# A perceiver layer with eight experts: conditional loads of the experts' low weight parts

## The reference

```python
expert_weight, expert_idx = jax.lax.top_k(probs, TOP_K)      # 2 of 8 experts for each of 2048 rows
...
binned = jnp.zeros((E, cap, Cc), x.dtype).at[sorted_e, local_pos].set(x[sorted_tok])
inter = jnp.einsum('ecd,efd->ecf', binned, w1_stack)
inter = jnp.square(jax.nn.relu(inter))
outb = jnp.einsum('ecf,edf->ecd', inter, w2_stack)
flat_out = outb[sorted_e, local_pos] * sorted_w[:, None]
moe_out = jnp.zeros((t, Cc), x.dtype).at[sorted_tok].add(flat_out)
return shared_out + moe_out
```

## Time and profile before

| | us |
|---|---|
| median of 3 runs (1295.1 to 1296.33) | 1295.25 |
| the profiled execution | 1296.94 |
| its span from first to last instruction | 1295.2 |
| TensorE busy | 1268.2 |
| VectorE busy | 749.9 |
| the routed groups, from about | 986 |
| to the last inner product of a group, about | 1230 |
| DMA traffic, whole kernel | 391.42 MB |

### The profile page before, as it was taken

The page is one execution under the profiler, slowest core; times in us unless marked ns, Lnnn a source line. Parts: engine busy times, 40 slices in busy tenths (PEclk is TensorE's granted clock), DMA queues, the critical chain, the costliest instruction groups (busy, mean ns, idle before and its releaser), DMA issues.

```text
span 1295.2 us, 21508 instructions
## 1 busy us (share of the span) xinstructions
PE 1268.2 (98%) x7571; PEld 829.1 (64%) x7572; DVE 749.9 (58%) x1404; ACT 358.0 (28%) x632; POOL 168.6 (13%) x173
## 2 busy tenths in 40 slices
PE   6999999999999999999999999999998999999999
PEld 3444444444444444467888888899986677777743
DVE  4456566554554545468878888666434444444456
ACT  2312212221121211326444444532312323223200
POOL 1000000000000000003100004504324000000054
PEclk9999999999999999999999999999999999999999
DMA  9999999999999999803467752223689898998897
GB/s 358 411 419 416 414 416 418 418 419 419 419 419 412 400 391 394 324 18 149 169 253 272 293 216 78 92 72 123 234 291 305 280 298 293 310 307 289 281 348 250
DMA packets 119699, 391.42 MB, mean 302 GB/s; under 512 B 11744, under 2 KB 34272, under 8 KB 115424
## 3 DMA queue, kind: packets, MB, share of 16 engines
q1 hardware_dynamic: 114528, 374.00, 76.3%
q0 software_dynamic: 5120, 16.78, 3.6%
HBM read 332.54 MB, written 58.20 MB: 302 GB/s over the span
## 4 chain that ended last, share of the span: by engine, by line
PE 92%; DMA 4%; DVE 2%; issue 1%; SPq 1%; ACT 0%; POOL 0%; ACTq 0%; POOLq 0%; DVEq 0%
PE ps L2016 14%; PE ps L1904 13%; PE ps L2088 12%; PE ps L2078 10%; PE ps L2371 5%; PE ps L1979 4%; PE ps L1862 3%; PE ps L2469 2%; PE ps L2461 2%; PE ps L2387 2%; PE ps L2390 2%; PE ps L2393 2%; PE ps L1994 2%; PE ps L2374 2%; DMA arena<-ctx_n 2%; PE ps L2377 1%
## 5 line engine op out<-in xcount | busy, mean ns | idle before, releaser
L2016 PE MATMUL ps<-arena 128*64 128x512 f32 (+1 forms) x832 | 192.3, 594 | 0.0
L1904 PE MATMUL ps<-arena 128*64 128x512 f32 (+1 forms) x1024 | 178.3, 504 | 1.8 <-DVE arena L1172 1.1
L2088 PE MATMUL ps<-split 128*128 128x256 f32 x1344 | 170.7, 285 | 1.2 <-DVE split L1371 1.2
L2088 PEld LDWEIGHTS ps<-split 128*128 128x128 f32 x1344 | 163.7, 191 | 5.7 <-issue 3.5
L799 ACT ACTIVATE arena<-ps 128x512 f32<-128x512 f32 (+2 forms) x132 | 67.3, 523 | 337.9 <-PE ps L1979 180.2
L1904 PEld LDWEIGHTS ps<-arena 128*64 128x64 f32 x1024 | 65.4, 137 | 122.2 <-issue 119.7
L2016 PEld LDWEIGHTS ps<-arena 128*64 128x64 f32 (+1 forms) x832 | 58.3, 137 | 112.4 <-issue 111.7
L1268 DVE SCALAR_TENSOR_TENSOR arena<-arena,hbar 128x512 f32<-128x512 f32 x128 | 90.5, 749 | 67.9 <-PE ps L1979 66.3
L2078 PE MATMUL ps<-split 128*128 128x512 f32 x384 | 96.7, 400 | 1.1 <-DVE arena L1439 1.1
L1242 DVE TENSOR_TENSOR F<-arena,ps 128x512 f32<-128x512 f32 x16 | 11.0, 688 | 135.9 <-ACT split L844 135.9
L702 POOL TENSOR_TENSOR arena<-arena,row_b 128x512 f32 (+1 forms) x16 | 20.2, 1268 | 474.0 <-DVE arena L1142 446.4
(11 more groups left out here) (245 smaller groups left out, 1995.9 us busy)
## 6 DMA issues: line engine op xcount, KB each, us to landing
arena<-ctx_t SPq DMA_DIRECT2D x122, 800.5 KB, 17.6
arena<-ctx_n SPq DMA_DIRECT2D x96, 768.0 KB, 14.1
arena<-ctx_n SPq DMA_DIRECT2D x32, 1024.0 KB, 15.5
split<-parts_low SPq DMA_DIRECT2D x26, 768.0 KB, 7.1
high<-parts_low SPq DMA_DIRECT2D x39, 512.0 KB, 4.9
moe_in<-zero SPq DMA_DIRECT2D x3, 3328.0 KB, 13.5
low_late<-parts_low SPq DMA_DIRECT2D x13, 768.0 KB, 7.0
moe_out<-arena SPq DMA_DIRECT2D x39, 256.0 KB, 4.5
```

What stands on the lines that cost most here:

```text
L1904: last = mm(bank(n)[S * h:S * (h + 1), 0:w], qT[:, k, S * h:S * (h + 1)], ctxT[h][:, k, at_j:at_j + w], start=(k == 0), stop=(k == KD - 1))
L2016: last = mm(bank(7)[S * h:S * (h + 1), :], ET[0:w, c, S * h:S * (h + 1)], ctxN[h][0:w, c, :], start=(c == 0), stop=(c == JC - 1))
L2088: last = mm(dst[:, 2 * P * m:2 * P * (m + 1)], w[a][:, k, c], tokens[b][:, k, :], start=(k + i == 0), stop=(k == KD - 1 and i == 2))
```

## The change

`load_low` and `load_low2` now take the group's number, and from group 3 on they give the DMA a condition: the expert of g differs from the expert of g - 3, which is the group that last used the same place. Where the two are equal the transfer moves nothing, and its semaphore is still counted up. The register loads move into the two functions, behind their waits. `load_low` also waits for the last transfer into its place.

```diff
+            def other_expert(g):
+                return expert_of(g) != expert_of(g - 3) if g >= 3 else None
+
+            def load_low(g):
+
+                i = g % 3
+                if g >= 3:
+                    sp.wait_ge(low_back[i], 16 * (g // 3))
                 sp.dma_start(low_w[i].bitcast(F32).rearrange("p k n -> p (k n)"),
-                             parts_low[0][bass.ds(e * P, P), :]).then_inc(low_back[i], 16)
-
-            def load_low2(g, e):
+                             parts_low[0][bass.ds(expert_of(g) * P, P), :], cond=other_expert(g)
+                             ).then_inc(low_back[i], 16)
+
+            def load_low2(g):
                 if g > 0:
                     sp.wait_ge(low2_back, 16 * g)
                 sp.dma_start(low_w2[g % 3].bitcast(F32).rearrange("p k n -> p (k n)"),
-                             parts_low[1][bass.ds(e * P, P), :]).then_inc(low2_back, 16)
+                             parts_low[1][bass.ds(expert_of(g) * P, P), :], cond=other_expert(g)
+                             ).then_inc(low2_back, 16)
...
                 if g + 1 < GT:
-                    e = expert_of(g + 1)
                     if g > 1:
                         sp.wait_ge(y_done, g - 1)
-                    load_low2(g + 1, e)
+                    load_low2(g + 1)
                 if g + 3 < GT:
-                    e = expert_of(g + 3)
                     sp.wait_ge(in_done, g + 1)
-                    load_low(e, g % 3)
+                    load_low(g + 3)
```

More of the change, by code:

```diff
@@ L588, in expert_of @@
                 return sp.value_load(eg_i[0:1, g:g + 1], min_val=0, max_val=E - 1)
-            def load_low(e, i):
+            def other_expert(g):
[4 more added lines that the diff above has]
+                    sp.wait_ge(low_back[i], 16 * (g // 3))
                 sp.dma_start(low_w[i].bitcast(F32).rearrange("p k n -> p (k n)"),
-                             parts_low[0][bass.ds(e * P, P), :]).then_inc(low_back[i], 16)
-            def load_low2(g, e):
+                             parts_low[0][bass.ds(expert_of(g) * P, P), :], cond=other_expert(g)
+                             ).then_inc(low_back[i], 16)
+            def load_low2(g):
                 if g > 0:
@@ L597, in load_low2 @@
                 sp.dma_start(low_w2[g % 3].bitcast(F32).rearrange("p k n -> p (k n)"),
-                             parts_low[1][bass.ds(e * P, P), :]).then_inc(low2_back, 16)
-            e = expert_of(0)
+                             parts_low[1][bass.ds(expert_of(g) * P, P), :], cond=other_expert(g)
+                             ).then_inc(low2_back, 16)
             sp.wait_ge(x3_out, 48)
-            load_low(e, 0)
+            load_low(0)
             load_w2(ARENA + KD * D, 7, 8)
@@ L620, in _ @@
             load_w2(2 * KD * D, 2, 3)
-            e = expert_of(1)
             sp.wait_ge(xgT_ready, 1)
@@ L627, in _ @@
             sp.wait_ge(shlo_used, 1)
-            load_low(e, 1)
-            e = expert_of(0)
+            load_low(1)
             sp.wait_ge(shared_done, TA)
-            load_low2(0, e)
-            load_low(expert_of(2), 2)
+            load_low2(0)
+            load_low(2)
             for g in range(GT):
                 if g + 1 < GT:
-                    e = expert_of(g + 1)
                     if g > 1:
                         sp.wait_ge(y_done, g - 1)
-                    load_low2(g + 1, e)
+                    load_low2(g + 1)
                 if g + 3 < GT:
-                    e = expert_of(g + 3)
                     sp.wait_ge(in_done, g + 1)
-                    load_low(e, g % 3)
+                    load_low(g + 3)
                     sp.wait_ge(xgT_ready, g + 2)
```

## The result

The changed kernel takes 1334.62 us (median of four runs, 1332.98 to 1335.87), the kernel before beside it 1295.28. The ratio is 1.0301, 95% interval 1.0283 to 1.0319: slower by 3%, 39.3 us. Lines have moved: L612 of before is L620 here, L648, L1675, L1786 and L1862 are L652, L1679, L1790 and L1866, and the two transfers of low parts, L591 and L597, are L598 and L605.

The account below looks back on a forecast made before the run. SyncE's queue, at 7.6 us per turn against TensorE's 6.31, was to bound the loop: 33 turns add 41.8 us, the start 2, the end gives back 2.2, 1.1 and 1.5, so +39 to 1334 us; range 1312 to 1354.

Parts of the forecast that it names:

- The turn: SyncE's loop: 4.89 us of own work plus 2.6 added, taken as 7.6 us per turn with slow instructions.
- slow single instructions: In SyncE's turn: 0.35 us of the mean 4.89; growing with the number of instructions, they make the turn 7.85.
- The ends: Around the 33 turns: start 2 us later; at the last group 2.2, 1.1 and 1.5 us given back.
- The clock: TensorE's clock in the loop was to stay at 1.00.
- rival 4: TensorE's clock falls in every group, making it 8.0 us: 13 us on top, 1347; chance 0.10 together with nothing skipped.
- the spare: SyncE's queue: 1.47 us of waiting per turn, own work 4.89 against TensorE's 6.31, so 1.42 us of room.
- rival 1: SyncE's queue keeps up, added work under 1.42 us per turn, no change: 1294 to 1297 us; chance 0.05.
- The register load's price: Register loads in SyncE's queue: 270 ns by the trace was used; the skill's 600 ns would give near +82 us.
- faster: The queue keeps up and group 3's rows come before TensorE needs them: 1291.5 us; chance 0.02.
- slow register loads: The four added register loads take 762 ns each: 65 us on top, 1399; chance 0.03.
- nothing skipped: Same instructions in SyncE's queue, but all bytes move: 1336 to 1345 us; chance 0.10 together with the falling clock.
- The 3.7 us at group 3: TensorE at group 3: 2.0 us standing plus 1.7 us lost clock, to be had if that load is skipped.

Follow-up runs that it names:

- experiment 1: The changed kernel with each group's expert number read once and kept, one register load per turn in place of six: 1294.22 us, ratio 0.9966.
- experiment 2: The kernel before with four unused register loads added per turn of SyncE's loop, all transfers whole: ratio 1.0305.
- experiment 4: The changed kernel with a condition that always holds, so every transfer moves its bytes: 1348.68 us, ratio 1.0384.
- experiment 3: The kernel before with two unused register loads added per turn of SyncE's loop, all transfers whole: ratio 1.0173.
- experiment 9: The kernel before, without condition, the transfers that the change skips cut to one of 128 rows by a table in the program: ratio 0.9957.
- experiment 10: The kernel before with rows issued ahead of the low part in the first turn alone: ratio 0.9989, in a second set of runs 0.9972.

## Why the prediction was right

**The bound.** SyncE's queue became the bound of the loop, as forecast; the time was 1334.62 against 1334, inside the range. Experiments 1 and 2 show the cause from both sides: with the register loads taken out of the changed kernel the loss is gone, and put into the kernel before they make one of its size, there with some waiting for rows in it that the changed kernel doesn't have.

**The turn.** 7.57 us against the 7.6 taken, from two terms that missed in opposite directions. A skipped transfer costs the queue 0.09 us, not the 0.34 of a full issue, so 25 skips gave back 6 us that I had not counted (the prediction had them as the free end of its range). What stood against it is the share of slow single instructions: the register loads cost 12.7 us above their median in the 33 turns, where in the kernel before they cost 3.7, so 0.27 per turn came with the added loads. (That is 0.11 per turn before the change, so slow loads are only a part of the 0.35 that the prediction put down to slow single instructions.) With the skips taken out, experiment 4 has turns of 7.85, the end of the range at which slow instructions grow with their number. The usual added register load was sized right: 269 ns and the same gaps. The comparison is an ALU_OP of 40 ns and a second FUSED_REGOPS; with gaps that is the 0.16 per transfer that was taken.

**The ends.** The timeline of VectorE and TensorE at the last group, beside the earlier trace rows:

```profile
1260.03 0.71 DVE L1679 STREAM_TRANSPOSE zero<-row_b 128x512 uint32<-128x512 uint32 x1 [4.07 <-DMA row_b<-moe_in]
1260.66 0.65 DVE L1790 TENSOR_TENSOR row_a<-row_a 128x512 f32<-128x512 f32 x1
...
1261.36 0.66 PE L1866 MATMUL ps<-ident,row_a 128*128 128x128 f32 x4 [0.16 <-DVE row_a L1790]
```

The start was 0.6 us later (1006.90 against 1006.26), not 2: the burst of group 3 was still 1.2 us later (994.02 against 992.78), but the low part ahead of it is skipped, its rows landed sooner, and the burst of group 4 was 1.6 us earlier (999.65 against 1001.24). From the last burst to the transpose of its rows it takes 1260.03 - 1256.75 = 3.3 us where it took 7.8, so 4.5 were given back against 3.3 in the sum (2.2 and 1.1); from the end of the square to TensorE's transposes 0.05 where it was 1.5, as taken. The sum as measured: 249.85 - 209.04 + 0.64 - 4.5 - 1.5 = +35.5, and the transposes of TensorE moved by 1261.36 - 1225.89 = 35.5. That is 3.5 less than the 39 put; the profiled execution took 1332.98 us, the fastest of the four, which is 36 more than its counterpart, and the median is 1.6 above it. So part of the closeness of 1334.62 to 1334 is luck.

**The clock.** Here the text was wrong in a detail. It said that the clock would stay at 1.00; it fell three times in the loop, for 3.4 us each. The first time:

```profile
1044.22 0.66 PE L1866 MATMUL ps<-ident,row_a 128*128 128x128 f32 x4 [1.65 <-DVE row_a L1790]
...
1046.00:1048.00 2.00, 2.00 (x6) 1.60 (x5) 0.03 (x1) 0.00 (x0) 0.00 (x0) 0.50 0.95 358
1048.00:1050.00 2.00, 2.00 (x6) 1.45 (x6) 0.00 (x0) 0.17 (x1) 0.00 (x0) 0.67 0.83 257
```

At 1044.22 TensorE had stood 1.65 us, and then shows 0.50, its lower level of 1.2 GHz. The other two falls came after it had stood 2.17 us (at 1074.99) and 2.92 us (at 1143.20). After 1.60 us (at 1173.54) and 1.98 us (at 1204.29) it stayed at 1.00, so the length of the last stop alone does not decide it. Over the loop the mean is 0.98, some 5 us of lost clock. As far as the turns show it cost nothing: they stayed at the queue's own 7.57, and by rival 4's arithmetic only what goes beyond the queue's turn could lengthen them.

**TensorE's busy share.** The prediction said some 83% in the loop; it is 90%. Between transposes of the same 33 groups, 1014.03 to 1261.36 us here and 1017.76 to 1225.89 before, both with 859 matmuls, the windows view counts 223.0 us busy against 208.1. Some 5 of the 15 us are the clock; where the rest comes from is not settled. The sum did not use this share.

**What was wrong: the spare.** The sum took 1.42 us per turn as room that the queue had, and rival 1 says that added work under it would cost nothing. Experiment 3 added 1.1 us and lost 22. The step that failed is reading a wait as spare: the wait for landed rows is set by the queue itself, because rows issued close behind a low part land late. A hint of it was in the earlier trace rows: the queue with room of experiment 1 waits mostly for the computation, and this one waited for its own rows alone and went no faster than TensorE. With all 2.7 us added, the queue's work was longer than any landing (at most 5.8 us from the start of a burst to its last piece, in a turn of 7.57), no such wait was left, and the turn was own work alone, so the forecast did not depend on it. A smaller change of the same kind would have been predicted wrong, as experiments 2 and 3 were.

**The register load's price.** 269 ns is the median of the 222 register loads in the changed kernel and 262 the least, 270 the median in the rows of before. The Trainium skill, page "DMA: Bandwidth & Descriptors", section "Latency and other measured facts", gives about 600 ns as the least for a `tensor_load`; the measurement decides against it for this form, and the estimate of near +82 us that followed from it did not come.

**The rivals.** No change and faster are out by the measured interval, slow register loads by the durations, nothing skipped by the bytes: 374.00 - 354.33 = 19.67 MB less, which is 15 x 1280 KB, the number of skips worked out from 39 groups and 8 experts. The 3.7 us at group 3 were there (experiments 9 and 10). The changed kernel had them for a moment, its transposes at 1007.41 us where they were at 1011.29, and could not keep them, since its queue was the bound from group 5 on.

## What to carry to other kernels

Skipping a transfer that nobody waits for gives little (0.3 to 0.4% here, from what its neighbours gain), and the instructions that decide on the skip stand in the queue's one line, and a queue that also brings the next rows can become the bound without a busy share ever showing it. Count its register work per turn beside the pace of the engine it feeds, read each value once, and keep it. A wait in such a queue is spare only if what it waits for does not move when the queue is late: look at what is issued just ahead of it, and try the small, urgent transfer before the large one.

## What the runs showed of the hardware

A transfer whose condition fails still passes the queue, in 0.084 to 0.10 us against 0.33 to 0.38 for one that moves data, and counts its semaphore up. Pieces of rows of 64 KB each, issued right behind a 768 KB transfer, landed 3.5 to 4.5 us after their issue in the changed kernel, and in 1.8 to 2.0 us with a skipped one in front; where the second product's low part had been issued only 1.1 us before (experiment 3), they took up to 6.9 us. A register load from on-chip memory takes 0.27 us at the median, with single ones up to 1.1 (30 to 35 slow ones in 33 turns, whether those held 132 or 198), and with the two register instructions behind it, and the gaps between them, 0.56 us of the queue.
